# Node scores from normalised tiles as the stationary operand, and unrolled row gathers of the edge stream

## The reference, cut to what matters

```python
def gnn(h, w, edge_src, edge_dst, W_self, W_func, W_att):     # h = layernorm(x), 3125 x 256
    h_s = h @ W_self.T
    z = h @ W_func.T
    concat_z = jnp.concatenate([z[edge_src], z[edge_dst], w], axis=-1)
    e = leaky_relu(concat_z @ W_att.T, 0.01)[:, 0]
    m = segment_max(e, edge_dst)
    e_exp = exp(e - m[edge_dst])
    alpha = e_exp / segment_sum(e_exp, edge_dst)[edge_dst]
    agg = segment_sum(alpha[:, None] * z[edge_src], edge_dst)
    return h + relu(where(deg > 0, h_s + agg, h))
x = x + gnn(layernorm(x), edge_attr_64, src, dst, ...)
x = x + ffn(layernorm(x))                  # 8 experts, the best 2 of each node, SiLU(w1)*w3, w2
```

## Time and profile before

| | us |
|---|---|
| median of 3 runs | 1122.06 (1118.36 to 1122.4) |
| profiled execution, whole | 1120.73 |
| its span, first to last instruction | 1119.0 |
| prologue, until the first gather | 65.8 |
| edge stream, first to last gather | 65.8 to 594.2 |
| last node tiles and choice of experts | 594.2 to about 700 |
| experts | about 700 to 1119.0 |

### The profile page before, as it was taken

The page is one execution under the profiler, slowest core; times in us unless marked ns, Lnnn a source line. Parts: engine busy times, 40 slices in busy tenths (PEclk is TensorE's granted clock), DMA queues, the critical chain, the costliest instruction groups (busy, mean ns, idle before and its releaser), DMA issues. The chain is left out here.

```text
span 1119.0 us, 20188 instructions
## 1 busy us (share of the span) xinstructions
PE 836.7 (75%) x4316; PEld 681.7 (61%) x4317; DVE 577.0 (52%) x1865; ACT 589.4 (53%) x1472; POOL 612.4 (55%) x615
## 2 busy tenths in 40 slices
PE   4872788965766675866758711898999999999995
PEld 2421444554555564655646501897888889899995
DVE  4523444454545454545545478355655555555553
ACT  2321656776968888688888730342423243342321
POOL 0047777777777777777772030644545363545442
PEclk9786888987888797887979955899999999999998
DMA  9366666556555555554552142323243222222221
GB/s 277 114 203 183 181 200 192 137 139 205 140 141 139 131 139 139 143 141 132 158 140 72 62 167 78 108 44 112 34 113 109 44 33 43 33 38 33 43 39 23
DMA packets 76127, 128.75 MB, mean 115 GB/s; under 512 B 20812, under 2 KB 56161, under 8 KB 74929
## 3 DMA queue, kind: packets, MB, share of 16 engines
q0 software_dynamic: 30720, 69.90, 27.4%
q1 hardware_dynamic: 38137, 51.60, 14.0%
q10 hardware_dynamic: 7200, 6.56, 1.7%
HBM read 106.86 MB, written 17.86 MB: 111 GB/s over the span
## 5 line engine op out<-in xcount | busy, mean ns | idle before, releaser
L777 POOL DMA_INDIRECT early<-ztab,early x416 | 399.4, 960 | 192.6 <-issue 185.9
L1314 PE MATMUL bank<-split_w,operands 128*128 x1344 | 238.8, 327 | 2.7 <-DVE operands L1832 1.4
L1236 PE MATMUL bank<-early,W 128*128 128x258 f32 x832 | 232.6, 432 | 5.2 <-ACT W L984 5.2
L1314 PEld LDWEIGHTS bank<-split_w,operands 128*128 128x128 f32 x1344 | 216.1, 191 | 7.6 <-issue 5.5
L1236 PEld LDWEIGHTS bank<-early,W 128*128 128x128 f32 x832 | 171.6, 215 | 53.7 <-issue 17.6
L984 ACT ACTIVATE W<-early 128x128 f32<-128x128 f32 x416 | 171.0, 482 | 37.2 <-PE bank L1236 31.2
L825 POOL DMA_INDIRECT out_rows<-late,row_ix x56 | 88.9, 1588 | 163.1 <-DVE late L1859 105.7
L1201 PE MATMUL bank<-ident,early 128*16 128x128 f32 x104 | 25.0, 390 | 162.6 <-DVE early L1571 162.6
L1054 ACT ACTIVATE late<-bank 128x384 f32<-128x384 f32 x56 | 27.5, 490 | 200.2 <-PE bank L1314 200.2
L973 ACT ACTIVATE early<-iota_row,W 128x128 f32<-128x128 f32 x416 | 131.6, 387 | 0.0
L1201 PEld LDWEIGHTS bank<-ident,early 128*16 128x16 f32 x104 | 10.6, 123 | 174.6 <-DVE early L1571 94.7
(11 more groups left out here) (233 smaller groups left out, 1305.7 us busy)
## 6 DMA issues: line engine op xcount, KB each, us to landing
W<-in_experts SPq DMA_DIRECT2D x8, 2132.0 KB, 8.7
W<-in_wt SPq DMA_DIRECT2D x26, 512.0 KB, 4.8
early<-ztab,early POOLq DMA_INDIRECT x416, 2.9
early<-in_x SPq DMA_DIRECT2D x26, 128.0 KB, 2.2
early<-ztab SPq DMA_DIRECT2D x25, 128.0 KB
early<-late SPq DMA_DIRECT2D x25, 128.0 KB
out_rows<-early ACTq DMA_DIRECT2D x25, 128.0 KB, 2.1
ttab<-early ACTq DMA_DIRECT2D x25, 128.0 KB, 2.6
```

Of the source, the lines that this page charges most:

```text
L777: nc.gpsimd.indirect_dma_start(out=zg[:, k * KG + c, :], out_offset=None, in_=ztab, in_offset=bass.IndirectOffsetOnAxis(ap=src_here[:, k / ...
L1236: last = mm(ps[2 + k // 2 % 2][:, 0:ZR], prob_hot[:, k % 3, c * P:(c + 1) * P], zg[:, k * KG + c, :], start=(k % 2 == 0 and c == 0), stop= ...
L1314: last = mm(bank[:, 0:n], x[:, (k % 2 * KC + c) * P:(k % 2 * KC + c + 1) * P], split_w[:, bass.ds(at + (part + w + c * H), n)], start=(i = ...
```

## The change

Three things. **First, the node scores.** The transposed tile `hnT` becomes the stationary operand and the two vectors the moving one (`att_v`, 2 columns): `s_of(t)` gives both scores of the 128 nodes of a tile as columns, two matmuls for each tile, and stands in PE's order three turns behind `hn_T`. `s_copy` takes the four or fewer column pairs of a block to `rows` and to `scal_by_tile`. The transposes use four banks, not two. The spread of s2 over the partitions moves behind the loop: `s2_block` multiplies a column of s2, repeated 128 times as stationary operand, by the identity, 25 matmuls of 128 columns, and `s2_copy` takes them to `s2_row`. The DMA that copied row 1 of `s2_row` over row 0 is gone. **Second, the order of loads and stores** on SP, and with it where DVE and ACT handle the row marks and clear `acc`. **Third,** POOL's gathers of all 104 groups are written out, without a hardware loop.

```diff
--- before.py
+++ after.py
...
@@ -605,33 +605,34 @@
...
                     sp.dma_start(first_i, dst_ends[:, 0, :].to_broadcast([P, GROUPS])).then_inc(dst_in_now, 16)
-                    sp.dma_start(row_int[0:GROUPS, :, :], mark_rows).then_inc(dst_in_now, 16)
             sp.wait_ge(att_padded, 1)
-            sp.dma_start(att_pad[0:EF, GROUPS - 2:GROUPS - 1], att_edge).then_inc(weights_in, 16)
-            sp.dma_start(att_pad[EF:2 * EF, GROUPS - 1:GROUPS], att_edge).then_inc(weights_in, 16)
+            sp.dma_start(att_pad[0:EF, GROUPS - 2:GROUPS - 1], att_edge).then_inc(att_pad_in, 16)
+            sp.dma_start(att_pad[EF:2 * EF, GROUPS - 1:GROUPS], att_edge).then_inc(att_pad_in, 16)
+
+            def src_of(k, b):
+                sp.dma_start(src_here[:, k, :], src_batch[bass.ds(b, 1), :, :].rearrange("b p k -> p (b k)"))\
+                    .then_inc(batch_src_in[k], 16)
+            for k in range(AHEAD // BATCH):
+                src_of(k, k)
+
+            def vectors_load(n):
+                if n >= W_RING:
+                    sp.wait_ge(vec_used, n - W_RING + 1)
+                sp.dma_start(vec_in[:, n % W_RING, :], wt[n, :, :]).then_inc(vec_loaded[n % W_RING], 16)
+            for n, (a, m) in enumerate(BLOCKS):
+                sp.wait_ge(z_ready, 2 * (n + 1))
+                sp.dma_start(ztab[a:a + m, :].rearrange("(t p) c -> p t c", p=P), rows[:, a // P:(a + m) // P, :])\
+                    .then_inc(z_stored, 16)
+                if n < W_RING - 1:
+                    vectors_load(n)
+            sp.dma_start(row_int[0:GROUPS, :, :], mark_rows).then_inc(row_int_in, 16)
+            vectors_load(W_RING - 1)
             sp.dma_start(wfunc_sb[:, :, :], w_func_t.rearrange("(k p) c -> p k c", p=P)).then_inc(weights_in, 16)
             sp.dma_start(wself_sb[:, :, :], w_self_t.rearrange("(k p) c -> p k c", p=P))\
                 .then_inc(weights_in, 16)
             sp.dma_start(router_sb[:, :, :], router.rearrange("(k p) c -> p k c", p=P))\
                 .then_inc(weights_in, 16)
 
-            def vectors_load(n):
-                if n >= W_RING:
-                    sp.wait_ge(vec_used, n - W_RING + 1)
-                sp.dma_start(vec_in[:, n % W_RING, :], wt[n, :, :]).then_inc(vec_loaded[n % W_RING], 16)
-            for n in range(W_RING):
-                vectors_load(n)
-            def src_of(k, b):
-                sp.dma_start(src_here[:, k, :], src_batch[bass.ds(b, 1), :, :].rearrange("b p k -> p (b k)"))\
-                    .then_inc(batch_src_in[k], 16)
-            for k in range(AHEAD // BATCH):
-                src_of(k, k)
-            for n, (a, m) in enumerate(BLOCKS):
-                sp.wait_ge(z_ready, n + 1)
-                sp.dma_start(ztab[a:a + m, :].rearrange("(t p) c -> p t c", p=P), rows[:, a // P:(a + m) // P, :])\
-                    .then_inc(z_stored, 16)
-            sp.wait_ge(s1_psum, len(BLOCKS))
-            sp.dma_start(s2_row[0:1, :], s2_row[1:2, :]).then_inc(s2_whole, 16)
             sp.wait_ge(pool_consts, 8)
             sp.wait_ge(row_marks_ready, 2)
             for i in range(2):
...
@@ -779,7 +779,7 @@
...
-                run(pool, GROUPS, AHEAD, PEEL, [(0, gather)])
+                run(pool, GROUPS, AHEAD, GROUPS // AHEAD, [(0, gather)])
 
             def general():
                 pool.wait_ge(edge_score_ready, len(PARTS))
@@ -859,35 +859,33 @@
             def hnT_copy(t):
                 act.wait_ge(hnT_psum, t + 1)
                 nc.scalar.activation(hnT[:, :, t * P:(t + 1) * P],
-                                     ps[t % 2][:, 0:C].rearrange("p (c n) -> p c n", n=P), ACT.Copy)\
+                                     ps[t % 4][:, 0:C].rearrange("p (c n) -> p c n", n=P), ACT.Copy)\
                     .then_inc(hnT_ready, 1)
+
+            def s_copy(n):
+                a, m = BLOCKS[n]
+                act.wait_ge(s1_psum, n + 1)
+                two = ps[5 + n % 2][:, 0:m // P * 2].rearrange("p (t two) -> p two t", two=2)
+                nc.scalar.activation(scal_by_tile[:, a // P:(a + m) // P, 0], two[:, 1, :], ACT.Copy).then_inc(z_ready, 1)
+                nc.scalar.activation(rows[:, a // P:(a + m) // P, C], two[:, 0, :], ACT.Copy).then_inc(z_ready, 1)
 
             def s2_copy(n):
                 a, m = BLOCKS[n]
                 act.wait_ge(s2_psum, n + 1)
-                nc.scalar.activation(s2_row[:, a:a + m], ps[5 + n % 2][:, 0:m], ACT.Copy).then_inc(s2_spread, 1)
-
-            def s1_copy(n):
-                a, m = BLOCKS[n]
-                act.wait_ge(s1_psum, n + 1)
-                nc.scalar.activation(rows[:, a // P:(a + m) // P, C], ps[2 + n % 2][:, 0:m // P], ACT.Copy).then_inc(z_ready, 1)
+                nc.scalar.activation(s2_row[:, a:a + m], ps[2 + n % 2][:, 0:m], ACT.Copy).then_inc(s2_spread, 1)
 
             act.wait_ge(ones_set, 1)
-            for t in range(TILES + 4):
+            for t in range(TILES + 2):
                 if t < TILES:
                     root(t)
                 if 0 <= t - 2 < TILES:
                     hnT_copy(t - 2)
-                if t % 4 == 3 and t >= 7:
-                    s2_copy((t - 7) // 4)
-                if t % 4 == 2 and t >= 10:
-                    s1_copy((t - 10) // 4)
-            s2_copy(len(BLOCKS) - 1)
-            for n in (len(BLOCKS) - 2, len(BLOCKS) - 1):
-                s1_copy(n)
-            act.wait_ge(pool_consts, 8)
-            nc.scalar.activation(acc[:, :], zero_rows[:, 0:1].to_broadcast([P, (TILES + 1) * ZR]), ACT.Copy)\
-                .then_inc(ones_set, 1)
+                if t % 4 == 0 and t >= 8:
+                    s_copy((t - 8) // 4)
+            for n in range(TILES // 4 - 1, len(BLOCKS)):
+                s_copy(n)
+            for n in range(len(BLOCKS)):
+                s2_copy(n)
 
             def scores_copy(part):
                 n = PARTS[part][1] - PARTS[part][0]
@@ -896,6 +894,9 @@
                     act.wait_ge(w_back, part)
                 nc.scalar.activation(score_rows[0:n, :], ps[1][0:n, 0:G], ACT.Copy).then_inc(w_copied, 1)
             scores_copy(0)
+            act.wait_ge(pool_consts, 8)
+            nc.scalar.activation(acc[:, :], zero_rows[:, 0:1].to_broadcast([P, (TILES + 1) * ZR]), ACT.Copy)\
+                .then_inc(ones_set, 1)
 
             def share_of(j, k, r):
                 act.wait_ge(den_ready, j + 1)
@@ -1087,44 +1088,45 @@
 
             def hn_T(t):
                 pe.wait_ge(hn_ready, t + 1)
-                if t >= 2:
-                    pe.wait_ge(hnT_ready, t - 1)
-                transposed(ps[t % 2], rows[:, t, 0:C]).then_inc(hnT_psum, 1)
-
-            def s_block(n):
+                if t >= 4:
+                    pe.wait_ge(hnT_ready, t - 3)
+                transposed(ps[t % 4], rows[:, t, 0:C]).then_inc(hnT_psum, 1)
+
+            def s_of(t):
+                n = t * P // G
+                pe.wait_ge(hnT_ready, t + 1)
+                if t * P % G == 0 and n >= 2:
+                    pe.wait_ge(z_ready, 2 * (n - 1))
+                at = 2 * (t - n * KG)
+                for c in range(KC):
+                    last = mm(ps[5 + n % 2][:, at:at + 2], hnT[:, c, t * P:(t + 1) * P], att_v[:, c, :],
+                              start=(c == 0), stop=(c == KC - 1))
+                if t % KG == KG - 1 or t == TILES - 1:
+                    last.then_inc(s1_psum, 1)
+
+            for t in range(TILES + 3):
+                if t < TILES:
+                    hn_T(t)
+                if t == 2:
+                    pe.wait_ge(att_ready, 1)
+                if t >= 3:
+                    s_of(t - 3)
+            pe.wait_ge(bad_ready, 1)
+            mm(ps[7][0:1, 0:1], bad[:, 4:5], ones[:, 0:1], start=True, stop=True).then_inc(bad_psum, 1)
+
+            def s2_block(n):
                 a, m = BLOCKS[n]
-                pe.wait_ge(hnT_ready, (a + m) // P)
+                pe.wait_ge(z_ready, 2 * (n + 1))
                 if n >= 2:
                     pe.wait_ge(s2_spread, n - 1)
-                for c in range(KC):
-                    last = mm(ps[5 + n % 2][:, 0:m], v_both[:, c, :], hnT[:, c, a:a + m], start=(c == 0), stop=(c == KC - 1))
+                for i in range(m // P):
+                    last = mm(ps[2 + n % 2][:, i * P:(i + 1) * P], scal_by_tile[:, a // P + i, 0:1].to_broadcast([P, P]),
+                              ident[:, :], start=True, stop=True)
                 last.then_inc(s2_psum, 1)
-
-            def s1_columns(n):
-                a, m = BLOCKS[n]
-                pe.wait_ge(s2_spread, n + 1)
-                if n >= 2:
-                    pe.wait_ge(z_ready, n - 1)
-                for i in range(m // P):
-                    last = mm(ps[2 + n % 2][:, i:i + 1], s2_row[0:1, a + i * P:a + (i + 1) * P], ones[0:1, 0:1],
-                              start=True, stop=True)
-                last.then_inc(s1_psum, 1)
-
-            for t in range(TILES + 4):
-                if t < TILES:
-                    hn_T(t)
```

(37 more changed lines are left out.)

26 lines of the change are left out of this document (10 added, 16 removed).

## The result

The changed kernel takes 1105.15 us in the median of 4 runs (1101.13 to 1110.48), the kernel before beside it 1121.35: a ratio of 0.989 on record, 95% interval 0.985 to 0.993. The two medians lie 16.2 us apart, a ratio of 0.986, which the interval contains. The profiled execution took 1102.92 us, its span is 1101.2. 1105 was predicted.

What follows compares the result with a forecast made beforehand. POOL issuing gathers one after another was taken as the bound, so only gather 0's start counts: 1120.73 less 16.3 us, from earlier x and shorter PE turns, gives 1104.4, said as 1105; range for 8 in 10: 1096 to 1112.

Steps and rivals of the forecast that it cites:

- Bound by the issue of gathers: Stream: POOL issues 416 gathers one after another, 528.4 us, so time saved before gather 0 counts in full.
- Part 1: Prologue loads: row marks leave the queue ahead of x, saving 3.8 us; tile 7 at 14.0, turn 5 at 15.0.
- Part 2: PE's node loop: a turn of transposes and `s_of` costs 1.28 us at the low clock, 20 turns to 40.6.
- the lower bound of 1.14: PE's node loop: low-clock turn in us if more of the transposes is hidden, against 1.28 taken.
- Part 3: Work moved behind the node loop: check, spread of s2, attribute scores, marks and loads are covered, costed at zero.
- The check, the flag: End of node loop: last `bad_ready` check's flag is there at about 44, before POOL asks at 47; covered.
- the margin at gather 48: Start of stream: `weighted` 0 done at 121.2, gather 48 at 126.58, so 5.4 us before a slot is missed.
- The last store isn't held up: SP's queue: edge-attribute loads alternating with stores need 210 GB/s against 339 seen, so no delay; 1.5 us if one intervened.
- Part 4: POOL's stream: writing out the 240 looped gathers is worth zero, with a gain of at most 4.6 us.
- The sum: Whole kernel: gather 0 at 49.5, 16.3 us earlier, taken off 1120.73 gives 1104.4; median said 1105.
- The clock: Rival, node loop: PE's clock goes up, DVE sets 0.85 a turn, gather 0 at 39.4, 1095 us; 15%.
- Slots: Rival, start of stream: consumers over 5.4 us late make gather 48 wait; 1111 us if 6 us are lost; 10%.

Runs made afterwards that it cites:

- after_third: The changed kernel with nothing edited, run once more beside the kernel before on another chip: 1104.67 us against 1117.07, ratio 0.991.
- fill_one: The changed kernel plus one unused bf16 matmul of 512 columns in each node-loop turn, on the slower chip: ratio 0.997 to the kernel before.
- fill_two: The changed kernel plus two unused bf16 matmuls of 512 columns in each node-loop turn, on the slower chip: ratio 0.991 to the kernel before.
- loads_behind: The changed kernel with row marks, vectors and weights loaded only after the last store of z rows has landed: 1104.21 us, ratio 0.988 to the kernel before.
- loads_between: The changed kernel with the loads behind the last store moved between the table's stores, on the slower chip: ratio 0.994 to the kernel before.

## Why the prediction held, step by step

**Bound by the issue of gathers: right** in the first traces and on the other chip. The gain of 17 us at gather 0 is there at gather 415, and the stream is 527.8 us as before. On the slow chip the slots are the bound, through PE's late results.

**Part 1: right.** Tile 7 at 14.03 (14.0 said), turn 5 at 15.03 (15.0); undone alone it costs 5.25 us on the slow chip, more than the 3.8 taken; with one and the same order of the loads of x DVE got tile 7 anywhere from 12.56 (after_third) to 14.03 us.

**Part 2: mechanism and clock right, size off by 1.9 us.** The term is the turn, 1.28 said and 1.174 measured, near the lower bound of 1.14. The four `s_of` take 0.71, not 0.84. Three of them start 0.213 us apart, exactly as L1079's loads did; what the sum left out is that the first one's load runs while the transposes are still busy (15.30, with the transposes from 15.03), so that it takes only 0.07. The pair of transposes takes 0.46, with 0.44 said. Of the low clock fill_one and fill_two leave no doubt, but the rows it was inferred from could not have told why: in 22.2 to 25.6 PE also stood idle for 1.08 of 3.40 us, and the end of an `s_block` reaches into it. The loop, low without a gap, shows that idle time wasn't needed for it.

The Trainium skill, page "TensorE: Matmul & The Clock Gate", section on the clock gate, says that sustained matmuls lift the clock. Here 26 us of PE without a gap, in transposes and 2-column matmuls, didn't, and the same loop with two matmuls of 512 columns a turn did. The same page of the Trainium skill, section on LDWEIGHTS, prices a load at its columns over 1.2, an estimate of 0.107 us for 128. That is near the 0.11 us by which the records of `s_of` follow one another at 2.4 GHz (fill_two); at 1.2 GHz, the clock of this loop, they follow at 0.213.

**Part 3: cover right, one term missed.** The check, the flag, the marks, the spread (8.03 us, with the clock up after its first 4) and the later scores cost nothing, and the margin at gather 48 was 6.1 (5.4 said). "The last store isn't held up" was wrong, by 1.2 us against the trace before and by 2.0 against loads_behind: the text looked at the loads ahead of the last store and not at the 1.9 MB queued right behind it.

**Part 4: right.** No gain, no loss, in either kernel.

**The sum:** gather 0 at 49.5 said, 48.77 measured. Turns 1.9 less and store 1.2 more, so the 16.3 became 17.0 by two errors that partly cancel. That the median came out within 0.2 us of the 1105 said is luck: its four runs lie 9 us apart.

**Rivals.** The clock didn't go up; with two fillers it does, which is worth 3 us at gather 0 and not the rival's 10, since the fillers take back 0.44 of the 0.56 us that the clock saves in a turn. Slots: no, but on the slow chip yes, where the change is worth 8.7 us in place of 16.

## What to carry to other kernels

Find the resource that paces the long stage by its own timeline (here 415 steps of issue on POOL), then price only what decides when it starts; everything else may be traded away for that. When loads are moved off a critical load, look both ahead of and behind the store whose landing is waited for: what is queued behind it takes its DMA time as well. Moving those loads ahead of it only helps if they have landed by then (loads_between: 7.28 us from copy to gather); holding them back until it has landed did help (5.27). And state the ring's margin as a number, 6 us here: a core on which one engine's results come late can have none, and then an earlier start is only worth part of itself.

## What was not expected of the hardware

- A loop that keeps PE busy without a gap for 26 us with 128x128 transposes and 2-column matmuls stays at 1.2 GHz; with one bf16 matmul of 512 columns a turn it still does (turn 1.60 us), with two it is at 2.4 GHz and the turn, with more work in it, is shorter (1.05 us).
- One chip ran this kernel 12.7% slower with the same durations of the instructions in the rows: 99 of PE's some 570 recorded semaphore rises came over 1 us late there, 511 us together, up to 18 us, all between 78 and 720 us.
- 129 KB took 5.4 us to land with 1.9 MB queued behind it (4.7 on the other chip), 3.4 us there with nothing behind it until it had landed; with nothing behind it but the loads ahead of it still in transfer, 5.0 and 5.8 us.
